# An attention and mixture-of-experts kernel: overflow check from the weights, joint projection and router product, tanh gates, gelu in four parts

## The reference

```python
xn = layernorm(x)
p = xn @ Wv.T + bv                       # 16 heads of 8; q = k = v = p
s = softmax(q @ k.T / sqrt(8)) @ v @ Wo.T + bo
z = layernorm(xn) * ln_g + ln_b
w = top2(softmax(z @ rW + rb)), renormalised     # 8 experts
hid = gelu(z @ W1[e] + b1[e])            # 128 -> 256
mixed = sum_e w[e] * (hid @ W2[e] + b2[e])
out = x + s * silu(xn + mixed)
```

## Time and profile before

| | us |
|---|---|
| median of 3 runs (lowest, highest) | 654.75 (652.24, 656.18) |
| the profiled execution | 647.5 |
| its span, first to last instruction | 645.5 |
| PE busy | 582.8 (90%) |
| ACT busy | 547.7 (85%) |
| DVE busy | 237.8 (37%) |
| POOL busy | 156.7 (24%) |
| mean granted TensorE clock | 0.917 of 2.4 GHz |

### The profile page before, as it was taken

The page is one execution under the profiler, slowest core; times in us unless marked ns, Lnnn a source line. Parts: engine busy times, 40 slices in busy tenths (PEclk is TensorE's granted clock), DMA queues, the critical chain, the costliest instruction groups (busy, mean ns, idle before and its releaser), DMA issues.

```text
span 645.5 us, 11510 instructions
## 1 busy us (share of the span) xinstructions
PE 582.8 (90%) x4036; PEld 243.4 (38%) x4036; DVE 237.8 (37%) x677; ACT 547.7 (85%) x595; POOL 156.7 (24%) x172
## 2 busy tenths in 40 slices
PE   5668599979999996999999999999799979999976
PEld 5445142324433444443434343433434434323311
DVE  7555567613333331132222222222234434224323
ACT  2453589959998999799999999999789989999994
POOL 5335147777400000000000000005256000077300
PEclk9856589979999996799999999999589989999978
DMA  7125698765565443435334635333175436232101
GB/s 223 42 81 152 224 302 272 231 170 154 131 155 138 111 100 101 130 77 140 103 98 115 156 93 155 75 88 98 38 196 154 140 95 187 66 91 59 34 17 49
DMA packets 103883, 81.33 MB, mean 126 GB/s; under 512 B 51371, under 2 KB 95806, under 8 KB 103230
## 3 DMA queue, kind: packets, MB, share of 16 engines
q1 hardware_dynamic: 99726, 72.16, 41.3%
q0 software_dynamic: 4096, 8.40, 4.6%
HBM read 57.97 MB, written 28.32 MB: 134 GB/s over the span
## 4 chain that ended last, share of the span: by engine, by line
PE 67%; ACT 14%; DVE 7%; issue 7%; SPq 4%; DMA 1%; ACTq 0%; DVEq 0%
PE bank_v L1154 30%; PE pair L1142 14%; ACT exps L686 11%; PE bank_f L1200 9%; PE bank_f L1191 7%; PE bank_f L1171 1%; PE pair L1073 1%; DVE rows_in_sb L720 1%; SPq L467 1%; PE bank_f L1078 1%; DVE veps L725 1%; PE bank_f L1167 1%; SPq L468 1%; DVE o_ring L990 1%; ACT xn_tok L627 1%
## 5 line engine op out<-in xcount | busy, mean ns | idle before, releaser
L686 ACT ACTIVATE exps<-pair 128x1024 f32<-128x1024 f32 x512 | 487.6, 1050 | 49.6 <-PE pair L1142 31.1
L1154 PE MATMUL bank_v<-exps,v_tok 128*32 128x512 f32 x2048 | 281.7, 623 | 2.2 <-DVE o_turned L946 1.5
L1142 PE MATMUL pair<-q_ring,k_ring 26*128 26x512 f32 x1024 | 155.5, 510 | 13.9 <-ACT exps L686 8.7
L602 POOL DMA_INDIRECT rows_in_sb<-o_dram,dest_i x64 | 60.7, 948 | 372.8 <-DMA o_dram<-o_ring 336.0
L1142 PEld LDWEIGHTS pair<-q_ring,k_ring 26*128 26x128 f32 x1024 | 61.9, 186 | 113.2 <-ACT exps L686 71.2
L1200 PE MATMUL bank_f<-w_ring,pre 128*128 128x128 f32 x320 | 65.5, 334 | 11.7 <-DVE o_ring L990 6.2
L1200 PEld LDWEIGHTS bank_f<-w_ring,pre 128*128 128x128 f32 x320 | 48.6, 218 | 72.1 <-issue 40.8
L592 POOL DMA_INDIRECT z_dram<-pre,dest_i x64 | 64.2, 1003 | 40.8 <-DVE dest_i L909 21.7
L1191 PEld LDWEIGHTS bank_f<-zT,w_ring 128*128 128x128 f32 x320 | 42.5, 193 | 75.2 <-DVE pre L981 45.1
L981 DVE TENSOR_TENSOR pre<-bank_f,w_ring 128x256 f32<-128x256 f32 x80 | 33.9, 424 | 98.5 <-PE bank_f L1191 98.5
L1154 PEld LDWEIGHTS bank_v<-exps,v_tok 128*32 128x32 f32 x2048 | 41.3, 110 | 68.7 <-ACT exps L686 38.0
(11 more groups left out here) (130 smaller groups left out, 306.3 us busy)
## 6 DMA issues: line engine op xcount, KB each, us to landing
w_ring<-w_dram SPq DMA_DIRECT2D x80, 192.0 KB
w_ring<-w_dram SPq DMA_DIRECT2D x80, 129.0 KB, 2.1
q_ring<-p_dram SPq DMA_DIRECT2D x56, 104.0 KB
k_ring<-p_dram SPq DMA_DIRECT2D x56, 96.0 KB
z_dram<-s_tok SPq DMA_DIRECT2D x4, 1280.0 KB, 8.7
z_ring<-z_dram SPq DMA_DIRECT2D x80, 64.0 KB
o_dram<-o_ring SPq DMA_DIRECT2D x20, 256.0 KB, 2.3
p_dram<-pre SPq DMA_DIRECT2D x16, 256.0 KB, 2.9
```

The source lines that it names most:

```text
L602: pool.indirect_dma_start(rows_in_sb[:, (h * HT + i) % GATHER_RING, c, :], None, o_dram[h][:, :], bass.IndirectOffsetOnAxis(dest_i[:, h, c ...
L686: nc.scalar.activation(exps[:, g % ES, 2 * half:2 * half + 2, :], pair[(2 * g + half) % 3][:, :, :], ACT.Exp, scale=SCALE).then_inc(exp_do ...
L1142: ins = nc.tensor.matmul(pair[h % 3][:, j % 2, :], k_ring[32 * j:32 * j + KROWS, n % 2, kt * P:(kt + 1) * P], q_ring[32 * j:32 * j + KROWS ...
L1154: ins = nc.tensor.matmul(bank_v[32 * j:32 * j + 32, :], v_tok[:, (n // HG) * KT + kt, first:first + 32], exps[:, g % ES, j, :], start=(kt ...
```

## The change

- **The check moves to the front.** The limit is tested on a bound from the weights alone: from Wv (and bv), each row's sum of absolute products within its head (`sum_gram`, `keep_m2`). TensorE decides before its prologue, which stands in both branches; SP and VectorE read the value at their old places. The maxima of the norms are gone, and a selector of -0.5 makes the halves.
- **The joint product.** Wv and the router weights lie side by side, 136 columns; four products a block (`rows_p`) give p by tokens and logits at once, in place of the router products and the transposes back. VectorE adds bv and keeps the logits.
- **Order and buffers.** VectorE's first normalisation has five passes instead of four; both second ones stand after all blocks. The first four heads are loaded together after block 2's store; W1 and two broadcasts are loaded after block 3. GpSimd's memsets of the key ring and the zeros are done by ScalarE. The halves of p lie in rings of two, p itself in a ring of four; the halved norms lie in the exps' buffers, so ScalarE waits for their stores ahead of steps 2 and 3.
- **Gelu in four parts.** Ups begin in step 36. After each five quads: five gelus of 128 x 1024, and six downs in a row, the rest spread. The gelus stand in steps 62, 109, 156 and 203 (before: 81 and 174, with ten quads each).
- **Tanh gates.** silu(y) is y (1 + tanh(y/2)) / 2: eight tanhs of four tiles each on ScalarE, sum and product on VectorE (`gate`), the half in `finish_y`. The gather ring has four tiles instead of six.

```diff
-M2_LIMIT = 400.0
-M2_LIMIT_BITS = int(np.float32(M2_LIMIT).view(np.int32))
+N2_LIMIT = 400.0
+M2_LIMIT_BITS = int(np.float32(0.99 * N2_LIMIT / (D + 1) / 2).view(np.int32))
...
-NORMS = ((0, 4), (4, 4), (8, 8), (16, 16))
-WARM = (9, 8)
+NORMS = ((0, 4), (4, 4), (8, 8), (16, 8), (24, 8))
+WARM = (4, 6)
...
-GELU_QUADS = 2
-GATHER_RING = 6
+GELU_PART = 5
+GELUS = HALVES * QUADS // GELU_PART
+GATHER_RING = 4
...
-MOE_AT = 31
+MOE_AT = 36
...
-BURST = 2
+BURST = 6
+SILU_TILES = 4
...
+        downs = [("down", first + i // 4, i % 4) for i in range(8)]
+        uses[g] = downs[:BURST]
...
+    for c in range(GELUS):
+        first = c * GELU_PART
+        step, t = burst(first, t)
+        gelu.append(step)
+        for q in range(first + GELU_PART, first + 2 * GELU_PART):
+            if c + 1 < GELUS:
+                t = both("up", q, t)
+            if q - GELU_PART + 2 < first + GELU_PART:
+                t = both("down", q - GELU_PART + 2, t)
...
+                if g == 2:
...
+                    for j in range(4):
+                        load_head(0, 0, j, 0, kq_in[0])
+                        load_stabiliser(0, j, kq_in[0])
                 sp.wait_ge(n2_copied, g + 1)
...
+                if g == 3:
+                    sp.dma_start(w1_stage, W1.rearrange("e h f -> h e f")).then_inc(w1_staged, 16)
...
-            pool.memset(k_ring[:, :, :].bitcast(F32), 1.0).then_inc(ring_cleared, 1)
...
-            pool.memset(s_tok[:, :, :], 0.0).then_inc(zeros_ready, 1)
...
+            def gelu(c):
+                last = (c + 1) * GELU_PART - 1
+                act.wait_ge(bank_f_read, written("up", last, 3))
+                for q in range(c * GELU_PART, last + 1):
+                    part = pre[:, q % QUADS, :]
                     nc.scalar.activation(part, part, ACT.Gelu).then_inc(gelu_done, 1)
...
+            def tanh_half(c):
...
+                nc.scalar.activation(th[:, 0, :], part, ACT.Tanh, scale=0.5).then_inc(tanh_ready, 1)
...
+                if 2 <= g < 4:
+                    act.wait_ge(m_kept[g - 2], NB // 2 * 16)
...
+            def sum_gram():
+
+                dve.wait_ge(gram_mm, 1)
+                square = bank_g[0][:, 0:D]
+                link(nc.vector.tensor_copy(gram, square))
+                link(nc.vector.scalar_tensor_tensor(out=gram, in0=gram, scalar=-1.0, in1=gram, op0=ALU.mult, op1=ALU.min))
...
+            sum_gram()
             norm1(1, *NORMS[1])
+            keep_m2()
             router_weights()
             norm1(2, *NORMS[2])
             keep_p(0)
             norm1(3, *NORMS[3])
             keep_p(1)
             keep_p(2)
-            norm2(0)
...
+            keep_n2(0)
+            norm1(4, *NORMS[4])
+            for g in range(3, NB):
                 keep_p(g)
...
+                keep_n2(g - 2)
+            for g in range(NB - 2, NB):
+                keep_n2(g)
+            for h in range(HALVES):
+                norm2(h)
             dve.wait_ge(m2_ready, 1)
...
+                for t in range(TB):
+                    ins = nc.tensor.matmul(p_rows[:, t, 0:TW], xnT[:, g % 2, t * P:(t + 1) * P], wv_rw[:, :], start=True, stop=True)
+                ins.then_inc(p_mm, 1)
...
+            with pe.Else():
+                keep_warm(WARM[1])
+                prologue()
+                first_scores(0)
+                rows_p(NB - 1)
+                norms_p(NB - 3)
+                first_scores(1)
+                norms_p(NB - 2)
+                first_scores(2)
+                norms_p(NB - 1)
```

More of the change, by code:

```diff
@@ L119, in burst @@
             g += 1
-        uses[g] = [("down", first + k, i) for k in range(BURST) for i in range(4)]
+        downs = [("down", first + i // 4, i % 4) for i in range(8)]
+        uses[g] = downs[:BURST]
         at.update({what: g for what in uses[g]})
-        return g
+        t = g + 3
+        for what in downs[BURST:]:
+            t = max(t, place(what, t) + 1 - MOE_STEP) + MOE_STEP
+        return g, t
     for h in range(HALVES):
@@ L128, in timetable @@
     t = MOE_AT
[L129 to L141, removed]
+    for q in range(GELU_PART):
+        t = both("up", q, t)
+    gelu = []
+    for c in range(GELUS):
[4 more added lines that the diff above has]
+            if c + 1 < GELUS:
+                t = both("up", q, t)
+            if q - GELU_PART + 2 < first + GELU_PART:
+                t = both("down", q - GELU_PART + 2, t)
     uses[STEPS + 3] = [("turn", NU - 1)]
@@ L623, in normalise @@
             def normalise(g):
-                if g != 3 and g <= 4:
-                    act.wait_ge(norm_ready, (1, 2, 3, 3, 4)[min(g, 4)])
+                if (c := {first // TB: c for c, (first, _) in enumerate(NORMS)}.get(g)) is not None:
+                    act.wait_ge(norm_ready, c + 1)
                 for t in range(g * TB, (g + 1) * TB):
@@ L687, in _ @@
                                          scale=SCALE).then_inc(exp_done, 1)
-            for h in range(HALVES):
-                if SILU_AT[h] >= STEPS:
-                    silu(h)
+            for c in range(SILUS):
+                if SILU_AT[c] >= STEPS:
+                    tanh_half(c)
         @block.vector
@@ L1016, in beside @@
                         scale_w1(part)
+                for c in range(SILUS):
+                    if g == GATE_AT[c]:
+                        gate(c)
                 for n in range(NU - 1):
@@ L1033, in _ @@
                     read_bank(*use)
-            finish_y(NU - 1)
+            for c in range(SILUS):
+                if GATE_AT[c] >= STEPS + VLAG:
+                    gate(c)
+            for n in range(NU):
+                if n == NU - 1 or Y_AT[n] >= STEPS + VLAG:
+                    finish_y(n)
         @block.tensor
@@ L1206, in _ @@
                 if g < STEPS:
-                    scores(g, 0)
-                    scores(g, 1)
+                    for half in range(2):
+                        if 2 * g + half >= 3:
+                            scores(g, half)
                 if g >= VLAG:
```

289 lines of the change are left out of this document (154 added, 135 removed).

## The result

The changed kernel takes **654.45 us** (median of 20 runs, 652.55 to 655.93); the kernel before, measured beside it in 20 runs, takes 649.05 (644.56 to 659.24). The ratio is **1.0086**, 95% interval 1.0065 to 1.0107: slower by 0.9%, where 2.3% were forecast (670.0 against 654.75). The time itself lies inside the range of 648 to 680, near its lower end; the direction was right, the size not.

What follows compares the result with a forecast made beforehand. No one engine bounds everywhere; TensorE carries 67% of the path that ends last, ScalarE 14%. Terms 6.5 + 7.5 - 6.5 + 15 - 7 = +15.5 gave span 661, median 670 us, range 648 to 680.

Steps and rivals of the forecast that it cites:

- start, to step 4's exps: Up to TensorE's router count product: VectorE's and SP's chain brings it at 87.2 us, not 80.69; +6.5 (0 to +9).
- steps 4 to 7: Steps holding the bias products: they run at the low clock, 4.3 us each; +7.5 (0 to +9.8).
- first expert product: Moved from step 31 to 36: ScalarE's stall there goes; -6.5 (-7 to -3).
- gelu in four parts: Gelu windows: four parts lose 12.2 us each at a fallen clock, 49, against 32 for two; net +15.
- tanh for silu: Expert gates: eight tanhs costing 4.2 us replace two silus costing 11; -7 (-9 to -6).
- the jump: VectorE's own jump in the start's chain, after the two second norms: priced at 4.87 us.
- pass four: VectorE's fourth norm pass in the start's chain: forecast to end at 33.4 us.
- The median: Step from span to median: add 9.25 us, turning a span of 661 into a median of 670.
- bursts at full clock: Rival at the gelu bursts: clock stays at 2.4 GHz, 7.6 lost a part, -4 not +15, time 651; alone 0.12.
- Tanh did not load its table: Rival at the tanh gates: each tanh loads its table, 20 us more, time 690; chance 0.02.
- the exact way: Rival at the decision up front: it goes the exact way, hundreds of us more; chance 0.01.

Runs made afterwards that it cites:

- before_moe36: The kernel before with the first expert product at step 36 and not 31; span 643.2 us, ratio 0.9796 to the kernel before.
- gelu_two_parts: The changed kernel with gelu in two parts of ten groups again and eight down products in the burst; span 640.1 us, ratio 0.9824 to the kernel before.
- before_tanh: The kernel before with the tanh gates alone and the gather ring of four tiles; span 635.8 us, ratio 0.9885 to the kernel before.
- silu_back: The changed kernel with one silu for each half in place of four tanhs and gates; span 665.7 us, ratio 1.0162 to the kernel before.
- norm2_early: The changed kernel with VectorE's two second norms moved up behind the copy of block 1's norms; span 648.3 us, ratio 0.9986 to the kernel before.
- warm_count: The changed kernel with ten identity products on TensorE between the logits and the second half of step 3's scores; span 648.7 us, ratio 0.995.
- bias_late: The changed kernel with the four bias products in steps 8 to 11, not 4 to 7, and W1's scaling behind them; span 646.9 us, ratio 0.9894.
- bias_spread: The changed kernel with bias products in steps 7, 10, 13 and 16 and W1's scaling in 17 to 20; span 646.2 us, ratio 1.0011.
- joined: The changed kernel with gelu in two parts, second norms early, bias products three steps apart and identity products at a burst; span 630.8 us, ratio 0.9738.
- joined_later: As joined, with identity products also behind a burst and W2's copies behind the first expert products' loads on SP's queue; span 621.2 us, ratio 0.9573.
- joined_count: As joined, with the count product at step 6, not 3, and the router's exp and first scatters at step 8; span 629.3 us, ratio 0.9742.
- joined_more: As joined, with W2's copies at step 17, not 24, and seven identity products also behind a burst's last down; span 632.1 us, ratio 0.9725.

## Why the prediction was right in direction and wrong in size

The terms, measured between the same exps of the two traces unless a run is named:

| term | forecast | measured |
|---|---|---|
| start, to step 4's exps | +6.5 | +5.65 (87.10 against 81.45) |
| steps 4 to 7 | +7.5 | +7.8 (17.57 against 9.79) |
| step 8 to step 21 | 0 | +1.8 (26.88 against 25.10) |
| first expert product | -6.5 | -7.0 in the trace (the waits of 5.48 and 1.57), -7.6 in before_moe36 |
| gelu in four parts | +15 | +10.3 by the windows (44.5 - 32.6 - 1.6), +11.6 in gelu_two_parts |
| tanh for silu | -7 | -9.0 in before_tanh, -9.2 by silu_back |
| tail behind the last exp | 0 | -0.5 |
| sum | +15.5 | about +9, by the first figure of each row; the span says +7.7 |

The remaining 1.3 us are not assigned to a place.

- **Start: right.** The chain, its order and its end are as written, and norm2_early moves the count by what the chain says. The links as listed sum to 90.1, and 87.2 was a middle value below that; with the jump at its measured size they give 86.5. One sum has a gap: 25 + 4.9 + 2.4 is 32.3, and the 33.4 at which pass four ends holds 1.1 that no term names (it ended at 34.1). The jump was over-priced: it was taken from a place where two engines stood 4.87 us, and this one stands 1.28.
- **Steps 4 to 7: right**, at 4.39 a step against 4.3. The clock then stayed low for steps 8 to 10 as well, 1.8 us that the term did not hold.
- **First expert product: right**, at 7.0 to 7.6 where -7 was the far end of its own range.
- **Gelu: the mechanism right, the size wrong.** This is the first failed step, the largest: "I take the clock as falling again. Six downs then start until 2.5 + 5 x 1.66 = 10.8", and 12.2 lost each. The first down comes at 2.49 and the cold pitch is 1.67, as written. But the clock fell inside the burst and not ahead of it: one down at full speed in the first part, none in the second, two or three in the third and fourth, so the next exps start 11.5 to 12.7 after the load and not 12.8, and a part loses 10.5 to 11.8. Together that is 44.5 and not 49, and the two parts of before lost 32.6 and not 32, the second one more than the first.
- **Tanh: the second failed step**, "Eight tanhs of 512 columns at about 0.52 ... make 4.2". All eight were charged to the path at ScalarE's price, where the prediction's own first part says that TensorE sets the pace with 0.19 a step over on ScalarE. For the four that stand in such steps before_tanh shows nothing lost; for the four behind the last expert product the charge of 0.52 was right. So 2.1 of the 4.2 are hidden, and the term is -9 and not -7. The page "ScalarE: Activation LUTs" of the Trainium skill, in its section on table sets, has tanh in the set of exp. The trace agrees: of nine table loads after, one is at the start, two are at each gelu and none is at a tanh. Seven tanhs stand between exps; the eighth (431.95) stands behind the gelus, ahead of the load back, and says nothing on exp's set.
- **The median: the third**, "add 9.25 to speak of the median". It made 661 into 670. One profiled execution against three runs was no measure of the distance between the two. This moves the time and not the size of the change: 661 against 645.5 is 2.4%, as 670 against 654.75 is 2.3%.
- Among the rivals, bursts at full clock had its price of 7.6 a part right and did not happen; the runs show that identity products make it happen. Its sum was wrong: 31 - 32 - 1.6 is -2.6 and not -4, so its time was 652 and not 651. Tanh did not load its table, and the exact way was not taken.

The gelu and the tanh term erred to the same side: 15 - 11.6 + 9.0 - 7 = 5.4 of the 7.8 us.

## What to carry to other kernels

A price on an engine is a price on the path only where that engine sets the pace: read the pace of the stretch first, then charge a small operation against the other engine's slack. Here the same tanh cost nothing in one stretch and 0.52 us in another. A stop of ScalarE costs TensorE its clock too, and filling TensorE's wait with products that nothing reads gave back 15 us of 653 here (14.4 by the medians of two sessions, 654.45 against 640.08). When a kernel's runs spread over 2%, state a forecast as a ratio and don't carry the distance between one profile and three runs into it.

## What the runs showed of the hardware

- The granted clock fell from 1.00 to 0.50 in bias steps in which TensorE's records show no idle time: two adjacent steps with four products of one column (1.05 us each time) passed at full speed in warm_count, then the third took 1.87 for them; in bias_late three passed, then the fourth took 1.87. With three steps between them it stayed at 1.00 in bias_spread, joined and joined_later; in joined_count and joined_more it fell once in these steps, each time behind a wait of TensorE (2.20 and 0.43 us).
- A stand of TensorE of 1.58 us behind a busy burst was followed by some 10 us at 0.50 in joined; with seven identity products in its place the clock was 1.00 throughout (249.21 to 269.13 in joined_later).
- The kernel before and before_moe36 are the same up to step 30, and their profiles differ there: the four bias steps take 91.24 - 81.45 = 9.79 us, against 12.01 (80.48 to 92.49) with the last at 4.39. Where the clock falls in these steps differs between executions; that this makes the wide spread of the kernel before (644.56 to 659.24, against 652.55 to 655.93 after) fits its runs, where longer spans have the lower mean clock (643.4 at 0.919, 658.0 at 0.895 in the session of before_tanh), and wasn't tested.
- The same two copies of W2 took SP's queue 5.80 us in joined, 3.20 in joined_later and 22.01 in joined_more, where they stood behind two stores of 1280 KB.
